# Transposing a unit's exponentials one unit later in the attention loop of a four-layer graph kernel

## What is computed

```python
q, k, v = (proj(Wq, bq), proj(Wk, bk), proj(Wv, bv))
scores = jnp.einsum('bhqd,bhkd->bhqk', q, k) * SCALE
mask = (adj_matrix + bond_matrix)[:, None, :, :]
scores = scores * mask
attn = jax.nn.softmax(scores, axis=-1)
ctx = jnp.einsum('bhqk,bhkd->bhqd', attn, v)
ctx = ctx.transpose(0, 2, 1, 3).reshape(b, seq_len, EMBED_DIM)
return jnp.einsum('bse,fe->bsf', ctx, Wo) + bo
```

## Time and profile before

| | us |
|---|---|
| median of 3 runs | 2987.2 |
| lowest and highest run | 2986.61, 2988.67 |
| span of the profiled execution | 2986.1 |
| PE busy (23040 matmuls) | 2935.2 (98%) |
| PE weight loads busy | 2371.0 (79%) |
| DVE busy | 1879.2 (63%) |
| ACT busy | 1491.5 (50%) |
| POOL busy | 720.8 (24%) |

### The profile page before, as it was taken

The page is one execution under the profiler, slowest core; times in us unless marked ns, Lnnn a source line. Parts: engine busy times, 40 slices in busy tenths (PEclk is TensorE's granted clock), DMA queues, the critical chain, the costliest instruction groups (busy, mean ns, idle before and its releaser), DMA issues.

```text
span 2986.1 us, 63496 instructions
## 1 busy us (share of the span) xinstructions
PE 2935.2 (98%) x23040; PEld 2371.0 (79%) x23040; DVE 1879.2 (63%) x4154; ACT 1491.5 (50%) x2761; POOL 720.8 (24%) x1305
## 2 busy tenths in 40 slices
PE   8999999999999999999999999999999999999999
PEld 7888787887878878888788886888868888688886
DVE  3797427874278742887428874388643886438863
ACT  2883317833288232873228732387323873238622
POOL 0343003420134201342013420134201341014410
PEclk9999999999999999999999999999999999999999
DMA  5202212022120231101311113111222022220200
GB/s 175 93 2 93 91 58 93 2 92 111 49 83 13 81 131 38 74 34 60 135 48 61 54 50 124 61 48 59 62 108 78 30 73 69 87 81 27 83 8 14
DMA packets 95317, 204.29 MB, mean 68 GB/s; under 512 B 10512, under 2 KB 41616, under 8 KB 94992
## 3 DMA queue, kind: packets, MB, share of 16 engines
q1 hardware_dynamic: 93456, 195.76, 17.9%
q0 software_dynamic: 1536, 4.20, 0.4%
HBM read 136.75 MB, written 8.65 MB: 49 GB/s over the span
## 4 chain that ended last, share of the span: by engine, by line
PE 68%; DVE 14%; issue 11%; POOL 4%; ACT 3%; DVEq 0%; DMA 0%; POOLq 0%; ACTq 0%; SPq 0%
PE ps L1122 39%; PE ps L1310 8%; PE ps L1403 7%; PE ps L1288 4%; PE ps L1478 4%; PE ps L1339 4%; DVE junk L832 3%; POOL H L578 3%; DVE Z L790 2%; DVE stats L629 1%; DVE h L848 1%; DVE dn L841 1%; DVE h L866 1%; POOL nm L566 1%; PE ps L1162 1%
## 5 line engine op out<-in xcount | busy, mean ns | idle before, releaser
L790 DVE CUSTOM_DVE_ANT_0 Z<-ps,adjN 128x1024 f32<-128x1024 f32 x512 | 624.0, 1219 | 69.3 <-PE ps L1288 67.1
L1046 ACT ACTIVATE Z<-Z,nm 128x1024 f32<-128x1024 f32 x512 | 587.4, 1147 | 54.2 <-POOL nm L566 54.1
L1310 PE MATMUL ps<-ident,Z 128*128 128x128 f32 x4096 | 545.9, 276 | 19.4 <-ACT Z L1046 16.9
L1310 PEld LDWEIGHTS ps<-ident,Z 128*128 128x128 f32 x4096 | 458.6, 140 | 129.4 <-issue 59.7
L1288 PE MATMUL ps<-kS,qS 128*128 128x512 f32 x1024 | 370.2, 444 | 3.3 <-issue 3.3
L578 POOL TENSOR_SCALAR H<-adjN 128x128 fp32r<-128x128 f32 (+1 forms) x456 | 316.6, 694 | 0.0
L566 POOL TENSOR_TENSOR nm<-nm,minus 128x1 f32<-128x1 f32 x512 | 97.1, 190 | 646.9 <-DVE nm L790 642.1
L1122 PE MATMUL ps<-mh,adjT 128*128 128x256 f32 x1024 | 223.6, 379 | 0.8 <-issue 0.8
L1122 PE MATMUL ps<-v,P 128*128 128x257 f32 x1024 | 223.6, 379 | 0.0
L1122 PE MATMUL ps<-hT,t3T 128*128 128x512 f32 x512 | 221.0, 592 | 0.0
L1122 PEld LDWEIGHTS ps<-v,P 128*128 128x128 f32 x1024 | 193.8, 189 | 31.9 <-issue 3.8
(11 more groups left out here) (183 smaller groups left out, 5713.5 us busy)
## 6 DMA issues: line engine op xcount, KB each, us to landing
adjT<-adjT_in SPq DMA_DIRECT2D x8, 4096.0 KB, 13.0
adjN<-adj_in SPq DMA_DIRECT2D x8, 4096.0 KB, 17.6
adjT<-adjT_in SPq DMA_DIRECT2D x8, 2048.0 KB, 7.7
qS<-qhi SPq DMA_DIRECT2D x112, 128.0 KB, 2.1
qS<-qlo SPq DMA_DIRECT2D x112, 128.0 KB, 2.1
adjT<-adjT_in SPq DMA_DIRECT2D x8, 1536.0 KB, 12.0
xn<-x_in SPq DMA_DIRECT2D x8, 1024.0 KB, 5.7
out<-x SPq DMA_DIRECT2D x8, 1024.0 KB, 4.8
```

The lines of the kernel that those rows point to most:

```text
L790: dve.tensor_tensor_reduce(Z[:, u % ZS], ps[:, 2 * (u % 2):2 * (u % 2) + 2].rearrange("p a n -> p (a n)"), adjN[:, u // HEADS], SCORE_SCAL ...
L1046: act.activation(Z[:, u % ZS], Z[:, u % ZS], ACT.Exp, bias=nm[:, u:u + 1], accum_out=sm[:, u:u + 1]).then_inc(exps.sem, 1)
L1310: mm = pe.transpose(ps[:, turn_bank((u, s)), rows(a)], Z[:, u % ZS, rows(NT // 2 * s + a)], ident[:])
```

## The change

Step numbers of the transposes and of their copies go up by one, by a new constant `BEHIND` = 1: in step u PE transposes unit u - 1 (behind the scores of unit u + 2, the weighting and the extra projections, step 0 included), ACT copies unit u - 2 and DVE copies unit u - 3. The exponential of unit u stays in step u on ACT. The list `turns` is changed in the same way, so in phase 6 the output of a tile stands now between the halves of the units of phases 4 and 5, where it stood between those of phases 5 and 6. `BOTH` stays 5. `Z` gets a fourth buffer; `PTz` gets memory of its own, so that `adjT` is loaded again in two parts: tiles 0 to 3 as before, tiles 4 to 7 after the last transpose. The scratch area of the POOL queue's DMAs is set to 8192 bytes.

```diff
-    ZS = 3
+    ZS = 4
@@
         (adjT0, adjT1) = region([("adjT", [P, NT, N], F32)],
-                                [("PTa", [P, PTA, NT, P], F32), ("Z", [P, ZS, N], F32), ("PTz", [P, NT, P], F32)])
-        (adjT,), (PTa, Z, PTz) = adjT0, adjT1
+                                [("PTa", [P, PTA, NT, P], F32), ("Z", [P, ZS, N], F32)])
+        (adjT,), (PTa, Z) = adjT0, adjT1
+        PTz = sb("PTz", [P, NT, P])
@@
-        adjT_back = [signal(f"adjT_back{s}", 16) for s in range(3)]
+        adjT_back = [signal(f"adjT_back{s}", 16) for s in range(2)]
@@
-        BACK = (range(0, PTA), range(PTA, PTA + ZS), range(PTA + ZS, NT))
+        BACK = (range(0, PTA), range(PTA, NT))
+        BEHIND = 1
@@
-            if u < UNITS:
-                turns += [(u, 0), (u, 1)]
+            if 0 <= u - BEHIND < UNITS:
+                turns += [(u - BEHIND, 0), (u - BEHIND, 1)]
@@ SP
                 sp.wait_ge(*ctxs(b, NT))
                 stand(sp, waited_sp)
-                reload_adjT(2)
-                sp.wait_ge(*adjT_back[2](b, 16))
+                sp.wait_ge(*adjT_back[1](b, 16))
@@ DVE
-                    if 2 <= u < UNITS + 2:
-                        evacuate(u - 2)
+                    if 0 <= u - 2 - BEHIND < UNITS:
+                        evacuate(u - 2 - BEHIND)
@@ ACT
-                    if 1 <= u < UNITS + 1:
-                        evacuate(u - 1)
+                    if 0 <= u - 1 - BEHIND < UNITS:
+                        evacuate(u - 1 - BEHIND)
@@ PE
-                    if u == 0:
-                        transposes(u)
                     if u + 2 < UNITS:
                         scores(u + 2)
@@
-                    if 0 < u < UNITS:
-                        transposes(u)
+                    if 0 <= u - BEHIND < UNITS:
+                        transposes(u - BEHIND)
@@
-    nc = bacc.Bacc("TRN2", target_bir_lowering=False, num_devices=1)
+    nc = bacc.Bacc("TRN2", target_bir_lowering=False, num_devices=1, dynamic_dma_scratch_size=8192)
```

## The result

The changed kernel takes 3007.9 us (median of 4 runs, 3005.7 to 3009.5) against 2987.9 of the kernel before beside it: 1.0068 times as long, 95% interval 1.0053 to 1.0082. It is slower, by 20 us; the forecast was 21.7 us and 3008.9. Its profiled execution has a span of 3003.9 us (2986.1 before) and was the fastest of the four.

What follows compares the result with a forecast made beforehand. PE, 98% busy, was taken to set the pace. A graph: -0.2 + 1.92 + 1.2 = +2.92 us; eight: +23.4; with the start, -1.7: +21.7, giving 3008.9 us, range 3001 to 3016 (chance 0.65).

Steps and rivals of the forecast that it cites:

- The exponential's wait: Phase 2: transposes stop waiting for the exponential but wait for ACT's copy behind it; gain 0.03 us a tile, not 0.27.
- Rival A: The wait for the exponential is what PE pays and vanishes, -16.9 us: 2975.8 us; chance 0.13.
- The new wait in phase 6: Second four transposes wait for DVE's copy behind the output's addition: PE stands 0.32 us longer, once a tile.
- Rival B: The ring's shift isn't paid, no stalls in phase 6: 2991.1 us; chance 0.10.
- C: Rival: DVE becomes the bound from phase 3 to 7, each stall 0.50 us: 3022.3 us; chance 0.12.
- The tiles' sum: Middle tiles of the loop: six stalls, +1.92 us a graph, less 0.2 gained in phase 2; +14.0 us in all.
- The end of the loop: Transposes come back where nothing hides them: last projection to last weighting 6.9 us instead of 5.7, +1.2 a graph.
- PE's own and moves whole: Stage L1403 after the loop: claimed to shift with the loop's end without changing, 0 us.
- The start: Step 0 loses its transposes: 0.79 us gained in graphs 5 and 7, about 0.15 in graph 0; -1.7 us for the run.
- Parts at nothing: `adjT` in two parts, `PTz` at another address, smaller scratch area and fourth `Z`: each claimed to cost 0.
- 0.65 us of idle time covers it: DVE's `HT` behind the `adjT` reload: if the data came later, idle time would hide it; cost 0.

Runs made afterwards that it cites:

- two edits that take the wait away: Each in the changed kernel: `BOTH` = 4 instead of 5, 2989.0 us; or DVE's copy ahead of the addition in phase 7, 2986.5 us.
- the memory part alone: Kernel before with fourth `Z`, `PTz` in its own memory, `adjT` reloaded in two parts and scratch area 8192, without the shift: 2993.3 us, ratio 1.0020.
- the memory part with three parts: Kernel before with fourth `Z`, `PTz` in its own memory, scratch area 8192 and `adjT` reloaded in three parts, without the shift: 2987.7 us, ratio 0.9997.

## Why the prediction was right, point by point

- **The exponential's wait is worth 0.03 and not 0.27 a tile: right.** 1.77 against 1.80 us from scores to scores, and the new releaser is the one foreseen, ACT's copy behind the same exponential. "0.27 us each, about once a tile" was a mean of two kinds, though: 0.23 in phase 2, and 0.54 in step 6 of each graph, which I had not looked at and which gave nothing back either. That the copy's place in ACT's list tied the wait to the exponential is shown by the kernels with that copy ahead of it: both waits go. Rival A (2975.8) has fallen. The Trainium skill (Perfetto Trace Analysis, Optimization Strategy) has a repeated gap as a possible sign of too few buffers; here a fourth `Z` alone brought nothing (0.9997), it is necessary for the shift (1.067 without it), and with the three PSUM banks left as they are the order of the copies closed the gap.
- **The new wait in phase 6, 0.32 a tile: right in place, mechanism and size.** Scores follow the projection 2.66 us behind instead of 2.32, the tile is 16.90 where 16.88 was forecast, and two edits that take the wait away give 2989.0 and 2986.5 us. Rival B has fallen, and C with it: DVE's busy time in the tile fell from 15.01 to 14.91 us, and the delay stayed at one copy.
- **The tiles' sum, 12.8 us against 14.0.** In the kernel before one tile in each of graphs 0 to 6 takes about 16.96 instead of 16.59 us, since `Z` of unit 54 starts 0.31 us late. My count, made from one middle tile, hadn't it: 7 by 0.37 is 2.6 us, and without it the 48 tiles would be 15.4 us slower. These seven gaps are also the 2.2 us that the earlier trace rows put down to a transpose and that I read as waits for a `Z` buffer. That reading was wrong: the transposes that this `Z` waits for by the code, those of unit 51, ended in graph 3 at 1311.79, and `Z` started at 1312.83; in the kernel with the memory part alone, where it needs unit 50, over 4 us lie between, and the gap is the same. So `Z` buffers were no bound at all. The gap is absent after the change; its cause is open.
- **The end of the loop, +1.20 a graph: right to the hundredth** (6.93 forecast, 6.93 measured); the first matmuls of L1403 then follow 0.23 us sooner behind the last weighting, which I hadn't forecast: -1.8. "PE's own and moves whole" was not so: ahead of L1403 stands the last projection, for which PE waited 0.22 us for DVE's normalisation (L758) in graph 3 before. This now starts 2.39 us behind the start of the last weighting instead of 2.62, and PE doesn't wait.
- **The start, -6.5 for -1.9 (the -1.7 and the first tile's share of phase 2): mis-sized in this execution.** I had divided the graphs by one execution into those whose scores wait for keys and those whose scores don't. Which graphs these are changes from execution to execution: in graph 3 the last pieces of the keys for the first tile landed up to 4.8 us after their issue before, and within 3.0 after. The kernels with the shift and this order of the loop have 280.0, 286.3 (`BOTH` = 4) and 283.7 us (copy ahead of the addition) in this stretch, mean 283.3; those without it have 286.5, 284.3 (`BOTH` = 4), 285.2 (scratch area), 285.1 and 286.3 (memory part), mean 285.5. The difference of the means is -2.1 us, near the forecast. But the three values lie 6.3 us apart, so this agrees with -1.9 without confirming it; the rest of the -6.5 is taken for the spread of single executions. What sets the landing of the keys is open; the scratch area doesn't.
- **"Parts at nothing": wrong for `adjT`.** The step that failed is "0.65 us of idle time covers it". DVE's next work is covered, but `HT` has a second consumer, POOL, and POOL's additions stretch a later product on DVE. Alone it costs 5.9 us, in the changed kernel 1.9: `junk` has 100.2 us in all there, 1.8 more than before. There DVE's last `HT` ends up to 0.43 us late against the stage L1402, by the list of waits for `adjT` in 3 graphs. In the changed kernel with `BOTH` = 4 it is on time in all eight, with the same joint signal. Why `adjT` comes in time there is open. The scratch area, and the fourth `Z` and `PTz` at another address, are shown to cost nothing by the kernels with the scratch area alone and with `adjT` in three parts.
- **Setup, +1.8.** Not forecast. The changed kernel with `BOTH` = 4 and the memory part with three parts have 88.7 and 88.6 us there too, the latter without the shift, and the changed kernel with DVE's copy ahead has 87.3 with it, so it isn't the shift; that it is the spread of the first loads is only argued.

The errors of the start (-4.6), of the link to L1403 (-1.8) and of the tiles (-1.2) on one side, those of setup and `adjT` (+3.7) and of the end (+0.1) on the other leave 3.9 us of the span: 17.8 against the 21.7 of the sum. They are larger than what is left of them, so that the sum comes this close is in part luck; the tile and the loop's end are not. The profiled execution was the fastest of its four; by the medians the difference is 20.0.

## What to carry to other kernels

When a wait is to be removed, list every wait of the same instruction and of its ring partners, and ask which engine's queue position ends each: a unit of slack is worth something only if the next releaser moves too. After any shift in a ring of banks, go round once by hand and see who copies out the bank three uses back, in which place of that engine's list. A transfer that is "covered" has to be covered for every consumer, and a covered engine may still slow another by running later beside it. A wait that a view names is checked against the code: the 2.2 us for a transpose were put down to something that had ended a microsecond before.

## What the runs showed of the hardware

- A product of two SBUF tiles on DVE took 1.23 us alone and about 3.7 to 4.45 beside POOL's addition of 128x2048 elements; it ended 1.1 us behind POOL each time, so a late POOL is passed on almost one to one.
- The size of the scratch area of POOL's DMAs, set to 8192 bytes, had no effect that could be told (ratio 1.0003, 0.9994 to 1.0012).
